# Decoder of two post-norm layers: place of the fills of relative rows on GpSimd, and another ending of the gated feed-forward

## What is computed

```python
x = layernorm(x + L0_attn(x)); x = layernorm(x + L0_xattn(x, ctx)); x = layernorm(x + L0_ffn(x))
x = layernorm(x + L1_attn(x))          # 16 heads of 16, relative rows
x = layernorm(x + L1_xattn(ctx, ctx, x, mask))
x = layernorm(x + L1_ffn(x))

def L1_attn(h):
    q, k, v = proj(Wq, bq), proj(Wk, bk), proj(Wv, bv)
    idx = clip(pos[None, :] - pos[:, None], -20, 20) + 20
    attn = softmax((q @ k.T + einsum('bhqd,qkd->bhqk', q, rel_k[idx])) / 4)
    return (attn @ v + einsum('bhqk,qkd->bhqd', attn, rel_v[idx])) @ Wo.T + bo

def L1_ffn(x):                         # 256 -> 768 -> 256, integer weights / 127
    h = silu(x @ wg.T) * (x @ wu.T)
    return h @ wd.T
```

## Time and profile before

| | |
|---|---|
| runs of the kernel before | 837.55 us median of 3 (835.93 to 840.35) |
| the profiled execution, and its span | 838.66 us; 836.9 us |
| busy share of the span | PE 94%, DVE 78%, ACT 73%, POOL 51% |
| DMA | 115.05 MB, 119 GB/s of DRAM traffic over the span |
| chain that ended last | PE 41%, ACT 9%, DVE 6%, DMA 4%, POOL 2% of the span |

### The profile page before, as it was taken

How to read it: one execution, slowest core, us unless ns; L and a number is a source line. 1 busy time by engine, 2 the same in 40 slices (tenths; PEclk the granted TensorE clock), 3 DMA queues, 4 the chain that set the end, 5 groups by cost and what they waited for, 6 DMA issues and landing times.

```text
span 836.9 us, 20947 instructions
## 1 busy us (share of the span) xinstructions
PE 788.0 (94%) x6901; PEld 595.6 (71%) x6901; DVE 651.7 (78%) x2466; ACT 611.3 (73%) x1595; POOL 426.3 (51%) x459
## 2 busy tenths in 40 slices
PE   8998999999899988989998999999999999999996
PEld 7876777677667766767777777777676777676785
DVE  4997778889898767777776776785888889986667
ACT  4547887887885366887787878894999999984331
POOL 1264576666744145553545534224865666335763
PEclk9999999999999999999999999999999999999999
DMA  9301672122101458978879799875122222200001
GB/s 317 141 26 45 204 199 64 54 74 83 71 14 77 177 174 257 286 222 269 247 219 279 223 280 285 264 208 187 43 68 68 67 68 68 65 1 1 26 26 52
DMA packets 105393, 115.05 MB, mean 137 GB/s; under 512 B 29061, under 2 KB 94085, under 8 KB 105030
## 3 DMA queue, kind: packets, MB, share of 16 engines
q1 hardware_dynamic: 104724, 113.35, 43.1%
q10 hardware_dynamic: 562, 0.35, 0.2%
HBM read 48.09 MB, written 51.82 MB: 119 GB/s over the span
## 4 chain that ended last, share of the span: by engine, by line
PE 41%; ACT 9%; DVE 6%; DMA 4%; issue 3%; POOL 2%; SPq 1%; DVEq 0%; ACTq 0%; POOLq 0%
PE bank L1544 7%; PE bank L242 6%; PE bank L250 4%; PE bank L2267 4%; PE bank L1559 3%; PE bank L2253 2%; PE bank L2284 2%; PE bank L1528 2%; PE bank L1585 2%; PE bank L1595 2%; DMA dist<-skew_scratch 2%; PE bank L2319 2%; ACT bias_area L2600 2%; ACT Sx L1750 2%; ACT q_heads L1758 1%
## 5 line engine op out<-in xcount | busy, mean ns | idle before, releaser
L242 PE MATMUL bank<-x_feat,w_all_mats 128*128 128x256 f32 x384 | 92.7, 386 | 2.3 <-ACT q_full L358 0.6
L2996 POOL TENSOR_TENSOR bnd<-bnd,consts 128x60 f32<-128x60 f32 x64 | 18.1, 304 | 138.4 <-DMA bnd<-band_scratch 138.4
L242 PEld LDWEIGHTS bank<-x_feat,w_all_mats 128*128 128x128 f32 x384 | 70.6, 191 | 14.8 <-ACT rw L2642 3.8
L2600 ACT ACTIVATE bias_area<-bias_area,mq_two 128x256 f32<-128x256 f32 x128 | 66.5, 530 | 0.0
L1003 DVE COPY q_heads<-bank 128x512 f32<-128x512 f32 x64 | 41.9, 683 | 23.4 <-PE bank L717 23.4
L896 ACT ACTIVATE Sx<-Sx,mq 128x256 f32<-128x256 f32 x128 | 54.4, 497 | 5.4 <-DVE mq L995 5.4
L2776 DVE COPY q_heads<-bank 128x512 f32<-128x512 f32 x64 | 41.6, 685 | 20.0 <-PE bank L2267 20.0
L904 ACT ACTIVATE q_heads<-bank 128x512 f32<-128x512 f32 x64 | 37.7, 589 | 26.4 <-PE bank L717 26.4
L1750 ACT ACTIVATE Sx<-Sx,mq 128x256 f32<-128x256 f32 x128 | 54.3, 501 | 2.3 <-DVE mq L1848 2.3
L1856 DVE COPY q_heads<-bank 128x512 f32<-128x512 f32 x64 | 42.0, 684 | 17.0 <-PE bank L1544 17.0
L896 ACT ACTIVATE Pr<-Pr,mq 128x256 f32<-128x256 f32 x128 | 54.4, 502 | 0.9 <-DVE mq L995 0.9
(11 more groups left out here) (309 smaller groups left out, 2338.1 us busy)
## 6 DMA issues: line engine op xcount, KB each, us to landing
dist<-skew_scratch SPq DMA_DIRECT2D x64, 296.0 KB, 4.3
skew_scratch<-rw SPq DMA_DIRECT2D x30, 588.0 KB, 4.8
bnd<-band_scratch SPq DMA_DIRECT2D x64, 108.0 KB, 2.9
band_scratch<-bias_area SPq DMA_DIRECT2D x32, 162.0 KB, 3.3
band_scratch<-bias_area SPq DMA_DIRECT2D x32, 148.0 KB, 2.7
skew_scratch<-dist SPq DMA_DIRECT2D x4, 1024.0 KB, 7.9
context_values<-dist SPq DMA_DIRECT2D x8, 512.0 KB, 2.6
v_two<-context_values SPq DMA_DIRECT2D x8, 512.0 KB, 4.1
```

The lines of the kernel that those rows point to most:

```text
L242: last = pe.matmul(dst[:, m * S:(m + 1) * S], w[:, k, m * P:(m + 1) * P], rhs[:, k, :], start=(k == 0), stop=(k == FT - 1))
L2600: last = act.activation(rows_of(n, g)[:, t, :], rows_of(n, g)[:, t, :], ACT.Exp, bias=mq_two[:, n % 2, g, t:t + 1], scale=-1.0, accum_out= ...
```

## The change

In the self-attention only GpSimd's order changes, for batches from 1 on: `fill(b+1, 1)` goes from behind to ahead of the first round's mask, `fill(b+1, 2)` from the fourth round to ahead of the third round's mask, and `fill(b+2, 0)` from the first round of the next batch to ahead of the mask in the fourth.

In the feed-forward's end, `low_last` makes the last low part on VectorE; batch 5's sum is taken ahead of the last `hidden`, its statistics and moments behind, and its output by GpSimd (`out_kept`); VectorE puts batch 4's output ahead as well. TensorE finishes batch 6 before it completes batch 7, whose first half it makes while it waits. Batch 7 gets buffers of its own (`slot`), so its steps wait for no earlier batch.

```diff
@@ -1466,10 +1466,15 @@
...
             hid_two = [q_par[:, 1, i, :, :].rearrange("p k n -> p (k n)") for i in range(2)]
-            y_two, xn_two = (y_sb, at), (xn, rl_wide)
-            st_two, mv_two, ve_two, rstd_two = (st, f_st), (mv, f_mv), (ve, f_ve), (rstd, f_rstd_sb)
+            y_two, xn_two = (y_sb, at, Sx[:, 0, :, :]), (xn, rl_wide, Sx[:, 1, :, :])
+            st_two, mv_two = (st, f_st, Pr[:, 0, :, 0:6]), (mv, f_mv, Pr[:, 0, :, 8:10])
+            ve_two, rstd_two = (ve, f_ve, Pr[:, 1, 0, 0:TT]), (rstd, f_rstd_sb, Pr[:, 1, 0, 4:4 + TT])
             NG = B // 2 * HT
...
+            def slot(t):
+                return t % 2 if t < B - 1 else 2
...
@@ -1725,20 +1730,21 @@
...
                         down(2 * (n // HT) - 1)
-                pe.wait_ge(n_steps2, 4 * (B - 3) + 1)
                 pe.wait_ge(lo_made, NG - 2)
-                for t in (B - 2, B - 1):
-                    for tt in range(TT):
-                        down_steps(t, tt, range(HT - 2))
+                for tt in range(TT):
+                    down_steps(B - 2, tt, range(HT - 2))
                 pe.wait_ge(lo_made, NG - 1)
...
                     down_steps(B - 2, tt, (HT - 2,))
+                pe.wait_ge(n_steps2, 4 * (B - 3) + 1)
+                down_steps(B - 1, 0, range(HT - 1))
                 pe.wait_ge(lo_made, NG)
...
                 last.then_inc(d_mm, 1)
+                down_steps(B - 1, 1, range(HT - 1))
                 for tt in range(TT):
-                    last = down_steps(B - 1, tt, (HT - 2, HT - 1))
+                    last = down_steps(B - 1, tt, (HT - 1,))
                 last.then_inc(d_mm, 1)
...
@@ -1923,46 +1929,69 @@
...
-                def out_begin(t):
-                    step = Steps(dve, n_steps2, t, 4)
-                    i = t % 2
+                def out_sum(t):
+                    i = slot(t)
                     dve.wait_ge(d_mm, t + 1)
-                    ge(dve, xn_ready, t - 1)
+                    if t < B - 1:
+                        ge(dve, xn_ready, t - 1)
                     if t < B - 2:
-                        step(dve.scalar_tensor_tensor(
+                        last = dve.scalar_tensor_tensor(
                             out=y_two[i][:, :, :], in0=bank[4 + t % 4][:, :].rearrange("p (t f) -> p t f", t=TT),
-                            scalar=UNIT, in1=x_tok[:, t, :, :], op0=ALU.mult, op1=ALU.add))
+                            scalar=UNIT, in1=x_tok[:, t, :, :], op0=ALU.mult, op1=ALU.add)
                     else:
...
                                                             in1=x_tok[:, t, tt, :], op0=ALU.mult, op1=ALU.add)
-                        step(last)
-                    step.wait()
+                    last.then_inc(n_steps2, 1)
+                def out_rows(t):
+                    i = slot(t)
+                    dve.wait_ge(n_steps2, 4 * t + 1)
                     for tt in range(TT):
                         last = dve.bn_stats(st_two[i][:, tt, :], y_two[i][:, tt, :])
-                    step(last)
-                    step.hold()
+                    last.then_inc(n_steps2, 1)
+                def out_moments(t):
+                    i = slot(t)
+                    hold(dve, n_steps2, 4 * t + 2)
                     for tt in range(TT):
                         last = dve.bn_aggr(mv_two[i][:, tt, :], st_two[i][:, tt, :])
-                    step(last)
-                    step.wait()
-                    step(dve.tensor_scalar(ve_two[i][:, :], mv_two[i][:, :, 1], EPS, None, ALU.add))
-                    step.end()
+                    last.then_inc(n_steps2, 1)
+                    dve.wait_ge(n_steps2, 4 * t + 3)
+                    dve.tensor_scalar(ve_two[i][:, :], mv_two[i][:, :, 1], EPS, None, ALU.add).then_inc(n_steps2, 1)
+                def out_begin(t):
+                    out_sum(t)
+                    out_rows(t)
+                    out_moments(t)
...
-                    i = t % 2
+                    i = slot(t)
                     dve.wait_ge(rstd2, t + 1)
-                    ge(dve, stored[i], 16 * (t // 2))
+                    dve.wait_ge(xn_ready, t)
+                    if t < B - 1:
+                        ge(dve, stored[i], 16 * (t // 2))
                     for tt in range(TT):
...
+                def low_last():
+                    n = NG - 1
+                    dve.wait_ge(hi_sb, n + 1)
+                    dve.wait_ge(lo_made, n)
+                    dve.tensor_tensor(part_of(1, n, 0, PAIR), hid_two[n % 2], part_of(0, n, 0, PAIR), ALU.subtract)\
+                        .then_inc(lo_made, 1)
...
                 hidden(0)
-                for n in range(1, NG):
+                for n in range(1, NG - 1):
                     hidden(n)
...
@@ -1973,13 +2002,18 @@
...
                         out_begin(t)
-                    if n >= HT and n % HT == 4:
+                    if n >= HT and n % HT == 4 and t < B - 4:
                         out_begin(t + 1)
...
                         out_end(t - 1)
-                out_end(B - 3)
+                out_end(B - 4)
+                out_sum(B - 3)
+                hidden(NG - 1)
+                out_rows(B - 3)
+                low_last()
+                out_moments(B - 3)
                 out_begin(B - 2)
...
@@ -2065,8 +2099,19 @@
...
                     pool.wait_ge(n_steps2, 4 * (t + 1))
-                    pool.tensor_tensor(rstd_two[t % 2][:, :], ve_two[t % 2][:, :], neghalf[:, :], ALU.pow)\
+                    pool.tensor_tensor(rstd_two[slot(t)][:, :], ve_two[slot(t)][:, :], neghalf[:, :], ALU.pow)\
                         .then_inc(rstd2, 1)
+                def out_kept(t):
+                    i = t % 2
+                    pool.wait_ge(rstd2, t + 1)
+                    pool.wait_ge(xn_ready, t)
+                    ge(pool, stored[i], 16 * (t // 2))
+                    for tt in range(TT):
+                        last = pool.tensor_scalar(xn_two[i][:, tt, :], y_two[i][:, tt, :], mv_two[i][:, tt, 0:1],
+                                                  rstd_two[i][:, tt:tt + 1], ALU.subtract, ALU.mult)
+                    last.then_inc(xn_ready, 1)
...
@@ -2085,7 +2130,7 @@
...
                 normalise(B - 2)
-                for n in range(NG):
+                for n in range(NG - 1):
                     low(n)
...
@@ -2097,6 +2142,7 @@
...
                         out_inverse(t + 1)
+                out_kept(B - 3)
                 out_inverse(B - 2)
...
@@ -2132,7 +2178,7 @@
...
                     sp.wait_ge(xn_ready, t + 1)
-                    sp.dma_start(out[t].rearrange("(t p) f -> p t f", p=P), xn_two[t % 2][:, :, :])\
+                    sp.dma_start(out[t].rearrange("(t p) f -> p t f", p=P), xn_two[slot(t)][:, :, :])\
                         .then_inc(stored[t % 2], 16)
...
@@ -3051,27 +3097,27 @@
...
                             n = NQ * b + j
-                            if j == 0 and b < B - 1:
-                                fill(b + 1, 0)
-                            if j == 0 and b == 0:
+                            if n == 0:
+                                fill(1, 0)
                                 ff_inverse(2)
                                 ff_normalise(2)
-                            if j == 0 and b < B:
+                            if j == 0:
                                 add_biases(b)
-                            if j == 0 and b == 0:
+                            if n == 0:
                                 split_q(1)
-                            if j == 1 and b < B - 1:
-                                fill(b + 1, 1)
-                            if j == 3 and 1 <= b < B - 1:
-                                fill(b + 1, 2)
-                                fill(b + 1, 3)
+                                fill(1, 1)
                             if j == 1 and b >= 2:
                                 normalise(b - 2)
+                            if j == 0 and 1 <= b < B - 1:
+                                fill(b + 1, 1)
+                            if j == 2 and b < B - 1:
+                                fill(b + 1, 2)
+                            if j == 3 and 1 <= b < B - 1:
+                                fill(b + 1, 3)
                             if j == 3 and b < B - 2:
                                 split_q(b + 2)
-                            if j == 2 and b == 0:
-                                fill(1, 2)
-                            if 1 <= n <= NQ * B:
+                                fill(b + 2, 0)
+                            if n >= 1:
                                 mask_bands(n - 1)
...
```

## The result

The changed kernel takes 832.19 us (median of 6 runs, 829.64 to 835.08) against 838.57 of the kernel before in the same runs (6, 835.93 to 840.35): ratio 0.9926, interval 0.99 to 0.9952. That is 6.4 us less, where 8.05 (against the profiled execution) or 7.0 (against the median) were forecast; 832.19 lies inside the range and 1.6 above the predicted 830.6. The profiled execution took 831.37 us with a span of 829.5.

A forecast was written before the change was run, and what follows sets the result against it. TensorE was taken to bound the self-attention stage, a chain over four engines the end. 4.4 + 0.85 + 1.7 + 1.1 = 8.05 us off the profiled 838.66 gave 830.6 us; range 828.5 to 836.5.

The forecast's parts named there:

- The two waits named first: Self-attention: moved fills shorten TensorE's waits at turn_whole by 4.4 us and at rel_scores by 0.85 us.
- The clock's 1.7: Self-attention, 375.25 to 378.90 us: the clock's fall behind the longest wait goes with that wait, gaining 1.7 us.
- rival 1: Clock's fall not the wait's doing, or absent in other executions: gain 6.35 us, 832.3 us; chance 0.23.
- The end: End of the feed-forward: low part on VectorE and TensorE's new order close batch 6's bank 1.1 us earlier.
- The low part at GpSimd's price: End of the feed-forward: a last low part of 1.36 us instead of 0.69 would leave a gain of 0.7 us.
- Rival 2: End: the last inverse waits for a whole VectorE output step; end comes 0.65 us later, 831.25 us; chance 0.06.
- Rival 3: Self-attention: TensorE waits for distances or bands instead; half of 5.25 us comes back, clock unsure, 835.0 us; chance 0.20.
- Rival 4: SP's queue stays held by another wait, the store goes as late; only the end is won, 837.6 us; chance 0.06.
- Rival 5: GpSimd held at fill(b+2, 0), delaying mask and TensorE; each us beyond cover costs six, 849.6 us; chance 0.05.

The follow-up runs named there:

- quarter2_only: Kernel before, old end kept, with only quarter 2's fill moved ahead of the third round's mask: 832.09 us, ratio 0.9947.
- end_only: Changed kernel with the old order of fills, so only the new end differs from the kernel before: 835.28 us, ratio 0.9991.
- fills_only: Kernel before with the new order of fills and nothing else: 831.83 us, ratio 0.9955.
- hold_10: Changed kernel with ten repeats of fill(b+2, 0) ahead of the band mask at each of six boundaries: 867.42 us.
- third set: Runs on a different chip from the other sets: kernel before 837.14 us (11 runs), changed kernel again 830.30 (six), and some variants.
- wait_filled: Kernel before with 18, 7 and 14 useless transposes on TensorE in its three waits ahead of turn_whole: 838.14 us, ratio 0.9998.
- low_pool: Changed kernel with the last low part back on GpSimd and batch 5's inverse behind it: 832.36 us, one run.
- quarters01_only: Kernel before, old end kept, with the fills of quarters 0 and 1 moved and quarter 2 left in the fourth round: 837.11 us, ratio 1.001.
- hold_4: Changed kernel with four repeats of fill(b+2, 0) ahead of the band mask at each of six boundaries: 832.08 us.
- spread: Changed kernel with the feed-forward's norms of earlier batches spread over more steps: 830.16 us, ratio 0.99.
- order_old: Changed kernel with TensorE's old order of the last products and the wait for batch 5's sum ahead of all: 831.19 us, one run.
- spread_more: Changed kernel with the feed-forward's norms of odd batches spread over five steps: 828.86 us, ratio 0.9905.

## Why the prediction was right, and where it was off

- **Forecast, sign and mechanism: right.** The two waits named first were the gain, and they went as described: quarter 2 alone carries it (`quarter2_only`), through SP's queue and the copy into `rw`. Said 4.4 + 0.85 = 5.25; measured 5.0 between two profiles without a low clock in the stage (`end_only` and `fills_only`), 4.1 to 4.5 between their runs and those of before. That 832.19 lies in the range shows little by itself, since the range takes in four outcomes.
- **The clock's 1.7: right price, wrong place in the sum.** The fall cost 1.69 in that execution, 1.3 at 285 us, and 1.5 to 1.6 each in `hold_10`. The failed step is "if the wait goes, so should this", booked against the median. The changed kernel has executions with falls too, at other places: its own profiled one has one at 285 us, where before had none, and without it would have taken some 830.1 (831.37 - 1.3). 6.35 without this term, rival 1, gives 832.3, and 832.19 was measured; but this closeness is in part luck, as at like clock the runs of the third set differ by 5.5 and not by 6.35. There, with clocks of 0.996 and above in all six runs, after took 830.30. So 830.6 is the time of an execution with next to no fall, and 832.2 the median of six runs of which three have a clock of 0.994. `wait_filled` adds that in one pair of executions half of the fall was covered: without it the distances are late instead. Rival 1's argument against itself had a wrong reading: the fall begins 1.3 us behind the end of the wait (375.25 and 373.92), not 0.9.
- **The end: 1.1 said, 1.40 measured; mechanism right.** The low part took 0.69 us, as priced. Batch 6's last four products start 4.04 us after `hidden(22)` (820.23 - 816.19) where 826.55 - 822.11 = 4.44 was said. The wait for batch 5's sum stands further back now, so the products start 0.48 after `hidden(22)`, not 0.66; and 30 of them took 3.56 us, 0.119 each, not 0.126, a rate that had been read from a stretch with a longer first product (0.39) and the whole of the last one in it (0.28, where the next can follow after 0.12). So TensorE was hardly the late one: the low part ended at 820.17, 0.06 ahead of the products that use it, where 0.25 was said, and any later low part costs at once (`low_pool`). Behind the start of the sum 5.12 us, said 5.02. The low part at GpSimd's price was said to leave 0.7 of the gain; `low_pool` has 0.86.
- **Rival 2 (VectorE and GpSimd shut each other out at the end): no.** The last inverse took 0.82 against 0.79 before; batch 6's ends at 824.51, 0.62 ahead of the output that needs it (said 0.5). But the prediction's reason against it, that sharing costs 0.1 us, overlooked a row of before in which the two did meet (last section); the change takes that pair apart.
- **Rival 3 (the waits change their name): not in this kernel.** 0.4 us came back at line 2299 (0.7 before at its old number 2253) and 0.2 at line 2347, and neither in `fills_only`. It is what happened where TensorE was kept busy in its waits (`wait_filled`).
- **Rival 4 (the store goes as late as now): no.** It went 5 us earlier in the boundary (said: near 434 by the clock of before, which is 430.3 here; measured 430.39).
- **Rival 5 (GpSimd held ahead of the mask): the mechanism is real, the cover as well.** Said over 5 us; 5.65 in the trace; 5.4 by `hold_10`. Beyond it each us costs six, and the clock on top, which the prediction's price left out.

## What to carry to other kernels

Follow a wait back to the first engine that was free and did nothing about it: here a DMA queue that stood still for 5 us behind a copy of 0.9 us whose input was there, and moving that one instruction was the whole gain of the larger part. Take what a fall of the clock costs from the rows, but do not book it as won unless other executions show the fall in the same place; and ask what would be late next if it were gone. Ahead of a chain of several engines at the end of a kernel, look at the order on the engine that feeds it together with the step to be sped up: here the faster step won nothing under the old order, and 0.54 of the 1.40 us under the new one.

## What the runs showed of the hardware

- The granted clock fell to about 0.5 at every one of six waits of TensorE of 3.9 to 4.6 us (`hold_10`), and behind one of 2.10 us in the profiled execution of before; behind waits of 1.60 (before), 1.57 and 1.91 (`end_only`), 1.66 and 1.58 (`quarters01_only`) it stayed at 1.00. At 285 us the same idle time of 1.11 or 1.12 us stands in the thirteen profiles compared; the twelve transposes behind it took 1.57 or 1.58 us in eight of them (before, `fills_only`, `end_only`, `quarter2_only`, `hold_4`, `wait_filled`, `spread`, `order_old`), and with a fall 2.19 in after, 2.27 in `spread_more`, 2.62 in `quarters01_only`, 2.68 in `hold_10`, 1.72 in `low_pool`, where it begins later. Such a fall cost 1.3 us at 285 (2.9 in `low_pool`), 1.69 at 375. The Trainium skill ("TensorE: Matmul & The Clock Gate", "What's actually happening") says that the monitor runs free of the kernel's start; that the fall at 285 us comes and goes, though no change reaches back to there, agrees with it.
- An instruction of VectorE can last until GpSimd's beside it ends. In `low_pool` batch 5's `ve`, 128x2, took 0.99 us where it takes 0.17 at the end of after; it ends with GpSimd's subtraction of two SBUF tiles, 819.99 to 821.27. In the kernel before, batch 5's output took 1.70 us beside the last low part (826.23 to 827.59) where batch 4's, of the same form, took 0.73: one of its two instructions took 1.37 instead of 0.41. It cost nothing there, as VectorE then waited 0.68 for TensorE.

```profile
820.30 0.99 DVE L1964 TENSOR_SCALAR ffn_ve<-ffn_mv 128x2 f32<-128x2 f32 x1
```

```profile
819.99 1.28 POOL L2087 TENSOR_TENSOR glu_low_odd_last<-q_par,glu_high_odd 128x512 fp32r<-128x512 f32 x1 [1.29 <-ACT glu_high_odd L1824]
```

```profile
826.05 1.70 DVE L1959 TENSOR_SCALAR rl_wide<-at,ffn_mv,ffn_rstd 128x256 f32<-128x256 f32 x2
```

  The Trainium skill ("SBUF — State Buffer", "Who interferes with whom") has the two shut each other out for a whole instruction when VectorE's runs in a two-port mode, or has two SBUF inputs while GpSimd's reads SBUF. Both pairs agree with its first case, though no row here shows in which mode an instruction ran. Beside GpSimd's output of batch 5 in after (821.40 to 823.84), an instruction with one tile as input, batch 6's `ve` took 0.26: there it did not last until the end of GpSimd's.
